# A decoder layer on one core: the channel mix's output product in three passes of split operands, its norm applied by ScalarE

## The reference, cut to what matters

```python
x = layernorm(x, ln0_w, ln0_b)
for l in range(4):
    h = layernorm(x, ln1_w[l], ln1_b[l]);  hh = time_shift(h)
    ...                                     # xk, xv, xr: mixes of h and hh
    x = x + (sigmoid(xr @ Wr[l].T) * wkv(time_decay[l], time_first[l], xk @ Wk[l].T, xv @ Wv[l].T)) @ Wo[l].T
    h = layernorm(x, ln2_w[l], ln2_b[l]);  hh = time_shift(h)
    xk = h * cmk[l] + hh * (1 - cmk[l])
    xr = h * cmr[l] + hh * (1 - cmr[l])
    kf = square(relu(xk @ Wck[l].T))        # 1024 wide
    x = x + sigmoid(xr @ Wcr[l].T) * (kf @ Wcv[l].T)
```

## Time and profile before

| | us |
|---|---|
| median of three runs | 1932.72 (1932.12 to 1933.3) |
| the profiled execution | 1931.72 |
| its span in the trace | 1930.0 |
| recurrent part | about the first 742 of the span |
| mean granted TensorE clock | 0.967 of full speed |

### The profile page before, as it was taken

How to read it: one execution, slowest core, us unless ns; L and a number is a source line. 1 busy time by engine, 2 the same in 40 slices (tenths; PEclk the granted TensorE clock), 3 DMA queues, 4 the chain that set the end, 5 groups by cost and what they waited for, 6 DMA issues and landing times.

```text
span 1930.0 us, 25404 instructions
## 1 busy us (share of the span) xinstructions
PE 1797.8 (93%) x9624; PEld 1488.3 (77%) x9624; DVE 1270.9 (66%) x2075; ACT 819.3 (42%) x1263; POOL 2.6 (0%) x23
## 2 busy tenths in 40 slices
PE   2499999999999998888699999999999999999997
PEld 1277887777877775555588998888988898998886
DVE  6889999899998844899744445444444444444445
ACT  3555776666766542222233333333233323333333
POOL 0000000000000000000000000000000000000000
PEclk9699999999999999999789999999999999999999
DMA  3000000001001003111021000011010011001001
GB/s 109 6 23 17 12 30 32 6 28 39 1 12 49 1 1 105 42 42 35 10 76 34 33 33 10 24 33 33 33 33 0 33 33 33 33 29 42 1 1 39
DMA packets 35645, 56.96 MB, mean 30 GB/s; under 512 B 2997, under 2 KB 20850, under 8 KB 35058
## 3 DMA queue, kind: packets, MB, share of 16 engines
q1 hardware_dynamic: 35570, 55.95, 9.0%
HBM read 52.27 MB, written 3.67 MB: 29 GB/s over the span
## 4 chain that ended last, share of the span: by engine, by line
PE 49%; DVE 1%; ACT 0%; issue 0%; ACTq 0%; DVEq 0%
PE fbanks L1583 16%; PE fbank L1583 16%; PE fbank L1599 16%; DVE acc L1438 0%; DVE fst L1464 0%; PE fbank L52 0%; DVE xk L1462 0%; ACT acc L1554 0%; PE fbanks L1616 0%; ACT acc L1531 0%; DVE fmv L1467 0%; DVE fyy L1478 0%; DVE frstd L1479 0%; DVE fyy L1477 0%; ACTq L1263 0%
## 5 line engine op out<-in xcount | busy, mean ns | idle before, releaser
L1414 DVE TENSOR_TENSOR hf<-sil,fbanks 128x512 f32<-128x512 f32 (+1 forms) x128 | 79.3, 620 | 338.7 <-PE fbanks L1583 278.9
L1522 ACT ACTIVATE sil<-fbanks 128x512 f32<-128x512 f32 (+1 forms) x128 | 69.6, 544 | 448.8 <-PE fbanks L1583 448.8
L1599 PE MATMUL fbank<-wl,hh 128*128 128x256 f32 x896 | 251.9, 281 | 0.0
L1599 PE MATMUL fbank<-wh,hl 128*128 128x256 f32 x896 | 251.8, 281 | 0.0
L1599 PE MATMUL fbank<-wh,hh 128*128 128x256 f32 x896 | 251.8, 281 | 0.0
L1414 DVE TENSOR_TENSOR hf<-sil,fbank 128x512 f32<-128x512 f32 (+1 forms) x128 | 79.4, 621 | 153.7 <-PE fbank L1583 146.8
L715 PE MATMUL pair<-wcv,kf 128*112 128x256 f32 x768 | 176.1, 379 | 0.0
L1599 PEld LDWEIGHTS fbank<-wl,hh 128*128 128x128 f32 x896 | 170.1, 190 | 2.1
L1599 PEld LDWEIGHTS fbank<-wh,hh 128*128 128x128 f32 x896 | 170.0, 190 | 2.0
L1599 PEld LDWEIGHTS fbank<-wh,hl 128*128 128x128 f32 x896 | 170.2, 190 | 0.0
L1421 DVE TENSOR_TENSOR hl<-hf,hh 128x512 fp32r<-128x512 f32 (+1 forms) x256 | 158.1, 618 | 0.0
(11 more groups left out here) (219 smaller groups left out, 3354.5 us busy)
## 6 DMA issues: line engine op xcount, KB each, us to landing
raw<-in_w_gate SPq DMA_DIRECT2D x16, 512.0 KB, 3.8
raw<-in_w_up SPq DMA_DIRECT2D x16, 512.0 KB, 4.7
raw<-in_w_down SPq DMA_DIRECT2D x16, 512.0 KB, 5.6
raw<-in_w_ck SPq DMA_DIRECT2D x4, 1024.0 KB, 4.9
wcv<-in_w_cv SPq DMA_DIRECT2D x4, 768.0 KB, 4.4
raw<-in_ctx_t SPq DMA_DIRECT2D x4, 750.0 KB, 5.1
ct<-in_ctx_t SPq DMA_DIRECT2D x4, 750.0 KB, 5.0
x<-in_x SPq DMA_DIRECT2D x4, 448.0 KB, 6.5
```

The costliest lines, as they stand in the source:

```text
L1414: dve.tensor_tensor(hf[i][:, 0:w], sil[i][:, 0:w], bank[2 * i + 1][:, 0:w], ALU.mult).then_inc(hf_ready, 1)
L1522: act.activation(sil[f % 2][:, 0:w], bank[2 * (f % 2)][:, 0:w], ACT.Silu).then_inc(sil_ready, 1)
L1599: ins = pe.matmul(bank[4 + 2 * (t % 2) + i // 2][:, (i % 2) * C:(i % 2 + 1) * C], a[t % 2][:, f, i * P:(i + 1) * P], m[h][:, DOWN + f * C: ...
```

## The change

- The output product of the channel mix takes all eight tiles of `kf` in three passes of split operands: 24 fp32r matmuls per sequence in place of 6 fp32r and 6 fp32 ones. ScalarE makes four rounded copies `kfh` per item, VectorE four low parts `kfl`; `low_kf(s, 1)` stands ahead of `wkv_sums`, `low_kf(s, 2)` and `low_kf(s, 3)` behind it.
- `wcv` is split whole: one stage load of 1024 KB per layer in place of 256 KB, no direct load (768 KB), and the rounded copy and the subtraction are 2048 wide in place of 512.
- The second norm is applied by ScalarE: VectorE makes a shift (`set_shift(2)`) in place of the four operations of `normalise(2)`, and ScalarE applies it in four activations, between `normalise(1)` and `reciprocal0`.
- Buffers are shared: `diff` with `dk`, `mix_ck` with `ckl`, `kf` with `kfl`; `wkv_numerator` waits for the mixes for that reason, and `hidden` has one wait for `cv_done` at its first pair.

The core of the diff (declarations of tiles and semaphores left out):

```diff
-SPLIT = 2
+FT = F // P
...
-        wcvh, wcvl = sb("wcvh", [P, SPLIT * C], F32R), sb("wcvl", [P, SPLIT * C], F32R)
-        wcv = sb("wcv", [P, (F // P - SPLIT) * C])
+        wcvh, wcvl = sb("wcvh", [P, FT * C], F32R), sb("wcvl", [P, FT * C], F32R)
...
+        diff = dk
...
-                    ("cr", wcr, cr_done, 1), ("cv", wcv, cv_done, 2))
+                    ("cr", wcr, cr_done, 1))
...
-                if name == "cv":
-                    w = w[:, 0:SPLIT * C]
                 sp.dma_start(stage[:, 0:w.shape[1]], w).then_inc(stage_in, 16)
...
+            def set_shift(k):
+
+                dve.scalar_tensor_tensor(shift[k][:], mean[k], -1.0, rstd[k][:], ALU.mult, ALU.mult)\
+                    .then_inc(shift_ready[k], 1)
...
             def wkv_numerator(m):
 
                 du = rw[m % 2]
+                dve.wait_ge(mix1_ready, 6 * min(m + 2, STEPS))
+                if m:
+                    dve.wait_ge(mix2_ready, 4 * m)
...
-                dve.wait_ge(kfh_ready, SPLIT // 2 * m + j + 1)
-                dve.tensor_tensor(kfl[:, 2 * j:2 * j + 2], kf[j][:], kfh[:, 2 * j:2 * j + 2], ALU.subtract)\
+                dve.wait_ge(kfh_ready, FT // 2 * m + j + 1)
+                dve.tensor_tensor(kfl[j], kf[j], kfh[:, 2 * j:2 * j + 2], ALU.subtract)\
                     .then_inc(kfl_ready, 1)
...
                 if valid(s):
                     rsqrt(2, s)
-                    normalise(2, xn[2], chunk(s), xn_ready[2])
+                    set_shift(2)
...
                 if valid(s + 3):
                     rsqrt(1, s + 3)
-                    set_shift(s + 3)
+                    set_shift(1)
                 if valid(s):
-                    for j in range(1, SPLIT // 2):
-                        low_kf(s, j)
+                    low_kf(s, 1)
                 if valid(s + 2):
                     wkv_sums(s + 2)
+                if valid(s):
+                    low_kf(s, 2)
+                    low_kf(s, 3)
...
-            def normalise1(m):
-
-                act.wait_ge(shift_ready, m + 1)
+            def normalise(k, m):
+
+                act.wait_ge(shift_ready[k], m + 1)
...
                 act.wait_ge(ck_done, 4 * m + j + 1)
-                split = 2 * j < SPLIT
-                if m and split:
-
-                    act.wait_ge(kfl_ready, SPLIT // 2 * (m - 1) + j + 1)
-                if m and not split:
+                if m and j == 0:
 
                     act.wait_ge(cv_done, 2 * m)
...
-                if not split:
-                    return
                 act.wait_ge(square_done, 4 * m + j + 1)
-                if m and j == 0:
-
-                    act.wait_ge(cv_done, 2 * m)
-                act.activation(kfh[:, 2 * j:2 * j + 2], t[:], ACT.Copy).then_inc(kfh_ready, 1)
+                act.activation(kfh[:, 2 * j:2 * j + 2], t, ACT.Copy).then_inc(kfh_ready, 1)
...
                 if valid(s + 2):
-                    normalise1(s + 2)
+                    normalise(1, s + 2)
+                if valid(s):
+                    normalise(2, s)
                 if valid(s + 1):
                     reciprocal0(s + 1)
...
-                    for j in range(F // P):
-
-                        if i == 0 and j % 2 == 0 and j < SPLIT:
-                            pe.wait_ge(kfl_ready, SPLIT // 2 * m + j // 2 + 1)
-                        elif i == 0 and j % 2 == 0:
-                            pe.wait_ge(square_done, 4 * m + j // 2 + 1)
-                        if j < SPLIT:
-                            parts = [(a[:, j], w[:, j * C:(j + 1) * C]) for a, w in ((kfh, wcvh), (kfh, wcvl), (kfl, wcvh))]
-                        else:
-                            parts = [(kf[j // 2][:, j % 2], wcv[:, (j - SPLIT) * C:(j - SPLIT + 1) * C])]
+                    for j in range(FT):
+
+                        if i == 0 and j % 2 == 0:
+                            pe.wait_ge(kfl_ready, FT // 2 * m + j // 2 + 1)
+                        parts = [(a, w[:, j * C:(j + 1) * C])
+                                 for a, w in ((kfh[:, j], wcvh), (kfh[:, j], wcvl), (kfl[j // 2][:, j % 2], wcvh))]
```

More of the change, by code:

```diff
@@ L118, in rwkv_phase @@
         rstd = {k: sb(f"rstd{k}", [T, G]) for k in (0, 1, 2)}
-        shift = sb("shift", [T, G])
+        shift = {k: sb(f"shift{k}", [T, G]) for k in (1, 2)}
         h = {1: sb("h1", [P, CB, G, T1]), 2: sb("h2", [P, CB, G, T1])}
-        diff = sb("diff", [P, CB, G, T])
-        mixed = {n: sb("mix_" + n, [P, CB, G, T]) for n in ("k", "v", "r", "ck", "cr")}
+        mixed = {n: sb("mix_" + n, [P, CB, G, T]) for n in ("k", "v", "r", "cr")}
         kp = sb("kp", [P, CB, G, T1])
@@ L137, in rwkv_phase @@
         bb = sb("bb", [P, CB, G, T1])
-        ckh, ckl = sb("ckh", [P, CB, G * T], F32R), sb("ckl", [P, CB, G * T], F32R)
-        kf = [sb(f"kf{i}", [P, 2, G * T]) for i in range(4)]
-        kfh, kfl = sb("kfh", [P, SPLIT, G * T], F32R), sb("kfl", [P, SPLIT, G * T], F32R)
+        ckh = sb("ckh", [P, CB, G * T], F32R)
+        with nc.sbuf_tensor("mix_ck", [P, CB, G, T], FP32) as t:
+            mixed["ck"] = t
+        ckl = sb("ckl", [P, CB, G * T], F32R)
+        with nc.sbuf_tensor("kf", [P, FT, G * T], FP32) as t:
+            kf = [t[:, 2 * j:2 * j + 2] for j in range(FT // 2)]
+        t = sb("kfl", [P, FT, G * T], F32R)
+        kfl = [t[:, 2 * j:2 * j + 2] for j in range(FT // 2)]
+        kfh = sb("kfh", [P, FT, G * T], F32R)
         cth = sb("cth", [T, G, C])
@@ L148, in rwkv_phase @@
         wexp_done, w_ready = sem("wexp_done"), sem("w_ready")
-        w_in = {n: sem("w_in_" + n) for n in ("k", "v", "r", "o", "cr", "cv")}
+        w_in = {n: sem("w_in_" + n) for n in ("k", "v", "r", "o", "cr")}
         stage_in, whi_ready, wlo_ready = sem("stage_in"), sem("whi_ready"), sem("wlo_ready")
@@ L157, in rwkv_phase @@
         h_ready = {k: sem(f"h_ready{k}") for k in (1, 2)}
-        shift_ready = sem("shift_ready")
+        shift_ready = {k: sem(f"shift_ready{k}") for k in (1, 2)}
         mix1_ready, mix2_ready = sem("mix1_ready"), sem("mix2_ready")
@@ L224, in _ @@
                     w = io["w_" + n][l].rearrange("p b c -> p (b c)")
-                    t = tile if n == "cv" else tile[:].rearrange("p b c -> p (b c)")
-                    sp.dma_start(t[:, :], w[:, -t.shape[1]:]).then_inc(w_in[n], 16)
+                    sp.dma_start(tile[:].rearrange("p b c -> p (b c)"), w).then_inc(w_in[n], 16)
                     if l == 0 and n == "r":
@@ L264, in rsqrt, with normalise @@
                 after(did(dve.scalar_tensor_tensor(rstd[k][:], yy[k][:], -3.0 * C, y0[k][:], ALU.add, ALU.mult)))
-            def normalise(k, out, xc, done=None):
+            def normalise(k, xc):
                 for i in range(G):
[L268 to L273, removed]
-                return n
-            def set_shift(m):
-                dve.scalar_tensor_tensor(shift[:], mean[1], -1.0, rstd[1][:], ALU.mult, ALU.mult)\
-                    .then_inc(shift_ready, 1)
+                    n = did(dve.tensor_scalar(xc[:, i, :], xc[:, i, :], mean[k][:, i:i + 1], rstd[k][:, i:i + 1],
+                                              ALU.subtract, ALU.mult))
+                return n
+            def set_shift(k):
+                dve.scalar_tensor_tensor(shift[k][:], mean[k], -1.0, rstd[k][:], ALU.mult, ALU.mult)\
+                    .then_inc(shift_ready[k], 1)
             def first_norm(m):
@@ L286, in first_norm @@
                 rsqrt(0, m)
-                after(normalise(0, xc, xc))
+                after(normalise(0, xc))
                 dve.wait_ge(params_in, 48)
@@ L513, in norm_out @@
                                    bias=param(m, b, b_), scale=param(m, b, w)).then_inc(h_ready[k], 1)
-            def normalise1(m):
-                act.wait_ge(shift_ready, m + 1)
+            def normalise(k, m):
+                act.wait_ge(shift_ready[k], m + 1)
                 xc = x[:, (m % GROUPS) * G:(m % GROUPS + 1) * G, :]
                 for i in range(G):
-                    ins = act.activation(xn[1][:, i, :], xc[:, i, :], ACT.Identity, bias=shift[:, i:i + 1],
-                                         scale=rstd[1][:, i:i + 1])
-                ins.then_inc(xn_ready[1], 1)
+                    ins = act.activation(xn[k][:, i, :], xc[:, i, :], ACT.Identity, bias=shift[k][:, i:i + 1],
+                                         scale=rstd[k][:, i:i + 1])
+                ins.then_inc(xn_ready[k], 1)
             def out(m, which, dst, done, func=ACT.Copy, scale=1.0):
@@ L703, in channel_out @@
                     n = 0
[L704 to L713 removed]
+                    for j in range(FT):
[3 more added lines that the diff above has]
+                                 for a, w in ((kfh[:, j], wcvh), (kfh[:, j], wcvl), (kfl[j // 2][:, j % 2], wcvh))]
                         for a, w in parts:
                             ins = pe.matmul(pair[3][0:T, i // 2, (i % 2) * C:(i % 2 + 1) * C], a[:, i * T:(i + 1) * T],
[L716 removed]
```

(2 more changed lines are left out.)

5 lines of the change are left out of this document (2 added, 3 removed).

## The result

The kernel after takes 2025.03 us (median of four runs, 2024.46 to 2026.08) against 1932.76 us before (four runs): a ratio of 1.0475, 95% interval 1.0463 to 1.0488. It is 92 us slower; the forecast was 2026.0.

What follows compares the result with a forecast made beforehand. The prediction took a closed chain of DVE and ACT, not PE, as the bound. Additions of 86.3 us, clock 5 and tail 2 made +93 on 1931.7: 2025, or 2026 on the median's scale; range 2008 to 2046.

Steps and rivals of the forecast that it cites:

- the DVE and ACT chain: Loop from `difference` through DVE, statistics, ACT's norm, reciprocal and `h` to the next `difference`; said to set the pace.
- `low_kf`, 3.0 us per step: Three more `low_kf` on DVE around `wkv_sums`, 1.00 us each, paid in full; their ACT copies cost nothing.
- The norm, 1.96 us per step, and 0.7 in steps with `wckl`: Second norm's four ACT activations ahead of reciprocal and `h`: 1.96 us; waiting for a late shift adds 0.7.
- `wcv`, 3.8 us per layer: Wider ACT copy 1.29, one more `kfh` copy 0.95, wider DVE subtraction 1.58 us, all in the chain.
- The new wait: `wkv_numerator` on DVE waits for the mixes because `diff` shares the buffer of `dk`: 0.13 us, between 0 and 0.2.
- PE's pause and the clock: PE stops some 4 us per step for late `low_kf`; the halved clock then loses 2.3 us, between nothing and 3.4.
- the slack: From the last `low_kf` to `h`, PE's branch takes 7.0 us, ACT's 8.8: PE is 1.8 us ahead.
- The term of the sum: Clock loss beyond the slack in the loop: 0.5 us in each of ten steps, 5 us.
- The second rival: The clock makes PE the bound, losing 3.4 us in every step: 2046 us, chance 0.12.
- The tail, +2: Steps 13 to 16: late `low_kf`, shorter product gaining 1.5 to 1.8, last `low_kf` about 1, clock about 2: +2 us.
- the 2.7 before step 0: Ahead of the first loop step, without `low_kf`: norm 1.96 plus 0.7 us for the late shift.
- The four kinds of step: Ordinary and `decay` steps 5.1 us longer each, with `wcvl` 8.9, with `wckl` 5.8.

Runs made afterwards that it cites:

- e5: Kernel after with one pass (high by high) of three in the channel mix's output product, all waits kept: 2014.38 us.
- e2: Kernel after without the three late low parts; tiles 2 to 7 multiply the first low part instead, as many matmuls: 1978.65 us.
- e3: Kernel before with only the second norm moved to ScalarE, between the first norm and the reciprocal: 1963.85 us.
- e6: Kernel after with only 512 of the 2048 columns of `wcv` loaded, rounded and subtracted, as many products: 2012.84 us.
- e1: Kernel after with the second norm applied by VectorE again: 2015.72 us.
- e4: As e1, with thirty extra matmuls keeping PE busy ahead of its wait for the third low part: 1998.28 us.
- e7: Kernel after with thirty extra matmuls keeping PE busy ahead of its wait for the third low part: 2022.54 us.
- e9: Kernel before, reordered: ACT's first norm ahead of the second's statistics, `h` ahead of the reciprocal, PE's `channel_out` two and two around the transposes: 1925.77 us.
- e10: As e9, with four of the eight tiles of `kf` split instead of two: 1924.81 us.

## Why the prediction was right

**The bound.** That the DVE and ACT chain sets the pace, and PE doesn't though it is 93% busy, was read from the unequal steps. e5 shows it (PE's work taken away, no step more than 0.1 us shorter than its kind), and e2, e3 and e6 show it from the other side (work taken from or put into the chain, steps changed by its size).

**`low_kf`, 3.0 us per step.** Shown by e2: 2.98 us (45.13 - 42.15). The copies on ACT that were costed at nothing cost nothing: ACT still waits 4.05 us for the statistics at the step's end, where it was 4.32.

**The norm, 1.96 us per step, and 0.7 in steps with `wckl`.** Shown by e3 for both (2.0, and 0.65 more in the step with `wckl`). In the kernel after, ACT waits 1.35 us for the shift in that step, of a forecast 1.45, and the step grew by 5.9 us of a forecast 5.8:

```profile
662.13 2.08 ACT L523 ACTIVATE xn<-x,shift,rstd 112x256 f32<-112x256 f32 x4 [1.35 <-DVE shift L276]
```

**`wcv`, 3.8 us per layer.** The step with it grew by 9.1 - 5.2 = 3.9 us over the ordinary one. DVE's wait for the copy is 3.28 us where it was 0.99, and the subtraction takes 2.21 (695.95 to the `low_kf` at 698.16):

```profile
695.95 2.29 DVE L409 TENSOR_TENSOR wcvl<-raw,wcvh 128x2048 fp32r<-128x2048 f32 x1 [3.28 <-ACT wcvh L556]
698.16 1.08 DVE L400 TENSOR_TENSOR kfl<-kf,kfh 128x896 fp32r<-128x896 f32 x1
```

e6 undoes the 1.29 and the 1.58 of it and gives back 2.8; the weights' larger load was never late (the longest took 10.5 us to land; in the first layer it was issued at 93.0 us and read at 126.8).

**The new wait, 0.13 us between 0 and 0.2.** It measures 0.19: in the kernel after the mixes' last operation starts at 583.22 and lasts 1.27 for two, and `wkv_numerator` starts 1.38 us behind its start; before, the same pair stood 1.19 us apart. That is near the upper end of its bounds. The kernel after, then before:

```profile
583.22 1.27 DVE L315 SCALAR_TENSOR_TENSOR mix_ck<-dk,prm,h 128x448 f32<-128x448 f32 x2
584.60 1.09 DVE L368 TENSOR_TENSOR dk<-eu,v 128x896 f32<-128x896 f32 x1
```

```profile
553.87 1.27 DVE L317 SCALAR_TENSOR_TENSOR mix_ck<-diff,prm,h 128x448 f32<-128x448 f32 x2
555.06 1.08 DVE L367 TENSOR_TENSOR dk<-eu,v 128x896 f32<-128x896 f32 x1
```

**PE's pause and the clock.** The pause for the third low part is 4.4 us in most steps and 5.0 in those with `decay` (forecast 4), and the clock falls to 0.50 behind it. The loss per step is 1.1 to 2.4 us by e1 and e4 (forecast 2.3, between nothing and 3.4), the slack 1.8 (forecast 1.8). The term of the sum was too large: 5 us, for half a microsecond in ten steps. In the kernel after `h` waits for PE in three steps alone, by 0.72, 0.69 and 0.31 us; the idle time of DVE ahead of L303 is 6.86, 6.84 and 6.46 there, where it is 6.0 to 6.1 in other steps of their kinds. By these and the steps' lengths the clock costs about 2.1 us in the whole loop. In the other steps the loss stayed inside the slack. What sets the three apart in the trace is how long the clock stays down behind the pause: 5.4 to 6.1 us, and 2.8 to 4.6 in the other steps. Two ordinary steps with the same pause (4.40 us up to 184.84, 4.37 up to 563.64), the first of them one of the three; columns as above:

```profile
185.00:191.00 6.00, 6.00 (x29) 6.00 (x30) 4.78 (x9) 2.77 (x8) 0.00 (x0) 0.50 0.01 3
```

```profile
567.00:573.00 6.00, 6.00 (x55) 6.00 (x54) 1.62 (x6) 5.83 (x12) 0.00 (x0) 1.00 0.01 3
```

In the first PE runs at 0.50 for some 6 us behind the pause, in the second for less than 3.5. By the two spacings, 0.118 and 0.213 us, an estimate of the loss is 2.7 and at most 1.5 us, on either side of the slack of 1.8. Why the clock comes back sooner in one step than in another stays open. The second rival, 2046, took the same mechanism in every step at its upper bound. The Trainium skill's rule on it ("TensorE: Matmul & The Clock Gate", section "HAM oscillation") agrees with the rows on the direction, 0.50 behind a wait of 5.02 us; what it costs was decided by the branch beside it.

**The tail, +2.** This term was too small. From the difference of step 13 to the last addition of the recurrent part it is 117.95 us for 113.04, +4.9. Counted by the second difference of each step (L309 before, L307 now), the step from 13 to 14 takes 2.85 us more, the next one 1.79 less (forecast for the shorter product: 1.5 to 1.8), and the last item 3.85 more, of which the forecast had 1 for its last `low_kf`. The clock, forecast at about 2, was more than that. In e7, with the pause of the first of these steps filled and the clock at 1.00 behind it, that step takes 39.41 us for 40.51, 1.1 less. In the last item PE is at 0.50 in two stretches, in the product with `wcr` (6.49 us; 5.37 for the same product of the last item before), and again from 826 to 829 us, behind short waits for the last low parts:

```profile
803.11 6.49 PE L679 MATMUL pair<-wcr,mix_cr 128*112 128x256 f32 x16 [4.28 <-DVE cth L418]
```

```profile
826.00:829.00 3.00, 3.00 (x16) 3.00 (x15) 0.00 (x0) 0.00 (x0) 0.00 (x0) 0.50 0.00 0
```

The first is 1.1 us; the second, worked out from 3 us at half speed, some 1.5. On the other side, the `wcr` product of the item in between took 5.36 us for 5.93, so 0.6 of the 1.79 is clock too. By these the clock comes to about 3.1 of the 4.9. The other 1.8 lie in the late low parts and the shorter product; beside its clock the forecast of +2 left nothing for them, and it gave no figure for the delay in the first of these steps.

**What the sum leaves.** From step 0 to 13 the forecast was 83.6 without the clock (86.3 less the 2.7 before step 0) and 88.6 with it; measured are 618.21 - 531.45 = 86.8. By the last layer's steps the additions make 85.3 of that, and the clock about 2; the first layer's steps, which in the kernel before were 0.7 us longer than the last layer's, take something back. Before step 0 the forecast was 2.7, and it is 2.75. The parts of the sum are in the span: 0.8 at the start, which the prediction had not, 2.75, 86.8, 4.9 in the tail, and -2.4 in the two later phases, which the change doesn't touch: 92.8, of 2022.8 - 1930.0. The -2.4 are the same code in another run; the length of these phases differs by as much between the kernels run here (1186.6 to 1190.0 us), and its cause stays open. So the close agreement of 2026.0 and 2025.03 is in part luck: the clock in the loop was some 3 us too much and the later phases took back 2.4, against 1.7 too little in the steps' additions, 2.9 in the tail and 0.8 at the start. The four kinds of step themselves, 83.6 forecast and 85.3 measured, are not luck.

**Where the reasoning would have failed.** The prediction treats the additions as a sum, and this holds in the one direction that was asked for. It doesn't hold backwards: the norm costs 31 us on the kernel before (e3) and taking it out of the kernel after gives 9.3 (e1), since the late low parts have brought PE's branch, with its lowered clock, to within about a microsecond of ACT's, and in steps with `decay` past it (46.75 us in e1 for 46.04). With the pause filled, taking it out gives 2022.54 - 1998.28 = 24 us (e7, e4).

## What to carry to other kernels

Where steps of a loop differ in their work on one engine, compare their lengths before trusting a busy share: an engine at 93% can be the one with slack, and what is added elsewhere then counts in full. Follow both branches from the point where an addition lands to the point where they meet again, at the clock that each will have there, since taking one addition back pays only down to the other branch. And before work is moved to another engine, look whether moving it within its own engine's order takes it off the chain: that gave the only times below the kernel before's, by 0.4% (e9, and e10, which can't be told from it).

## What the runs showed of the hardware

Giving TensorE more to do made the program faster: thirty products per step in its pause raised the granted clock of the loop from 0.92 to 0.98 and took 17.4 us off (e1 to e4). The pauses they fill are 4.4 to 5.0 us long, and behind one of them the spacing of the same matmuls was 0.213 us instead of 0.118 for some 4.4 us (609.62 to about 614). Behind pauses of equal length the lower clock lasted differently long: some 6 us behind 4.40 us (to 191), less than 3.5 behind 4.37 us (to 567).

Two waits for work of its own engine aren't free on VectorE, though that work stands just ahead in program order: 0.19 us for the instruction that has them (1.38 against 1.19 us between the starts of L315 and L368).
